# Query and key projections of the first attention: padded stacks replaced by head rows spread through DRAM, with a new order of steps and of filler matmuls

## The reference, cut to what matters

```python
x = x + _L0_xattn_ref(_layernorm(x), ctx_512, ...)   # 16 heads of 8: causal self attention plus attention to the context, then @ Wp
x = x + _L0_ffn_ref(_layernorm(x), ...)              # 8 experts of 512 hidden units, top 2 by a router
x = x + _L1_xattn_ref(_layernorm(x), ctx_512, ctx_512, ...)  # one head of 128, to the context
x = x + _L1_ffn_ref(_layernorm(x), ...)              # 16 heads of 64, values and outputs mixed by top-2 gates over 8 experts
# in _L0_xattn_ref
q = _heads(x @ Wq + bq); k = _heads(x @ Wk + bk)                # self
qc = _heads(x @ Wcq + bcq); kc = _heads(cross_input @ Wck + bck)  # context
```

## Time and profile before

| | us |
|---|---|
| median of 3 runs (lowest, highest) | 1233.53 (1227.9, 1242.0) |
| the profiled execution, its own time | 1238.11 |
| its span | 1236.4 |
| TensorE busy in the span | 1127.7 (91%) |
| DVE, ACT, GpSimd busy | 698.5, 489.9, 84.1 |
| mean granted TensorE clock, as a share of full | 0.939 |

### The profile page before, as it was taken

One profiled execution on the slowest core, in us unless ns is written; L12 is line 12 of the kernel. 1 busy time (PEld: TensorE's weight loads), 2 busy tenths in 40 slices (PEclk: granted clock), 3 DMA queues, 4 the chain that ended last, 5 costly groups with the idle time before them and its releaser, 6 DMA issues.

```text
span 1236.4 us, 22167 instructions
## 1 busy us (share of the span) xinstructions
PE 1127.7 (91%) x8916; PEld 853.0 (69%) x8916; DVE 698.5 (56%) x1867; ACT 489.9 (40%) x1022; POOL 84.1 (7%) x246
## 2 busy tenths in 40 slices
PE   6989979899999999999989999999999999988786
PEld 4547745788569775887578856986578766875475
DVE  5513574856666566746585666747585657424400
ACT  4243406353544525452635344462536163422120
POOL 0020002000100001000200010000100010000000
PEclk9999968999999989999999988999999998998866
DMA  8000001041301421052103230052105210233322
GB/s 227 1 1 5 2 0 37 6 81 41 75 6 27 77 56 42 11 76 70 41 6 72 41 84 6 14 82 65 37 15 77 69 39 1 56 57 82 62 41 56
DMA packets 198037, 56.90 MB, mean 46 GB/s; under 512 B 173569, under 2 KB 193839, under 8 KB 197935
## 3 DMA queue, kind: packets, MB, share of 16 engines
q1 hardware_dynamic: 195630, 51.20, 21.4%
q10 hardware_dynamic: 2304, 4.29, 1.1%
HBM read 31.36 MB, written 24.12 MB: 45 GB/s over the span
## 4 chain that ended last, share of the span: by engine, by line
PE 72%; DVE 11%; ACT 7%; DMA 4%; SPq 3%; issue 3%; ACTq 0%; DVEq 0%
PE bank L985 11%; PE bank L830 9%; PE bank L794 9%; PE bank L900 5%; PE bank L574 5%; PE bank L941 4%; PE bank L720 3%; PE bank L735 3%; PE bank L968 2%; PE bank L645 2%; DMA at<-at_d 2%; PE bank L681 2%; DVE negmax L1322 2%; ACT pa L1079 2%; ACT hi_part L1065 2%
## 5 line engine op out<-in xcount | busy, mean ns | idle before, releaser
L1322 DVE TENSOR_REDUCE negmax<-bank 128x2 f32<-128x512 f32 (+1 forms) x224 | 138.9, 682 | 55.0 <-PE bank L681 35.6
L1079 ACT ACTIVATE pa<-bank 128x512 f32<-128x512 f32 x224 | 123.4, 596 | 109.2 <-PE bank L735 75.9
L1096 ACT ACTIVATE pa<-bank,b_c 128x256 f32<-128x256 f32 x256 | 106.9, 470 | 108.9 <-PE bank L794 106.7
L985 PE MATMUL bank<-vb,pb 128*128 128x65 f32 x1024 | 131.9, 292 | 3.2 <-issue 2.0
L985 PEld LDWEIGHTS bank<-vb,pb 128*128 128x128 f32 x1024 | 128.0, 207 | 9.3 <-ACT pb L1158 3.5
L794 PE MATMUL bank<-xnT_a,w 128*128 128x256 f32 x512 | 124.0, 385 | 1.7 <-ACT pa L1096 1.3
L830 PE MATMUL bank<-w,pa 128*128 128x128 f32 x1024 | 124.2, 276 | 0.0
L830 PEld LDWEIGHTS bank<-w,pa 128*128 128x128 f32 x1024 | 121.9, 192 | 3.2
L574 PE MATMUL bank<-ident 128*128 128x512 bf16 x417 | 117.8, 411 | 0.0
L1158 ACT ACTIVATE pb<-bank 128x512 f32<-128x512 f32 x128 | 69.7, 599 | 111.8 <-PE bank L945 110.8
L794 PEld LDWEIGHTS bank<-xnT_a,w 128*128 128x128 f32 x512 | 92.1, 190 | 17.3 <-ACT pa L1096 4.9
(11 more groups left out here) (241 smaller groups left out, 1715.9 us busy)
## 6 DMA issues: line engine op xcount, KB each, us to landing
v_d<-at SPq DMA_DIRECT2D x32, 256.0 KB, 3.3
vb<-v_d SPq DMA_DIRECT2D x32, 256.0 KB, 5.6
at_d<-at SPq DMA_DIRECT2D x32, 256.0 KB, 2.1
at<-at_d SPq DMA_DIRECT2D x32, 256.0 KB, 4.5
pv_d<-pvs SPq DMA_DIRECT2D x8, 512.0 KB, 2.8
pvs<-pv_d SPq DMA_DIRECT2D x16, 256.0 KB, 4.3
w<-in_L_ffn_W_dram ACTq DMA_DIRECT2D x1, 2048.0 KB, 9.5
bd<-mix_d SPq DMA_DIRECT2D x128, 8.0 KB
```

Source lines behind the costliest of these rows:

```text
L985: mm = pe.matmul(BB[2 + qt][:, i * (DH + 1):(i + 1) * (DH + 1)], pb[:, h % NPB, kt * T + qt * P:kt * T + (qt + 1) * P], vb[:, kt, h, :], s ...
L1079: nc.scalar.activation(pa[:, e % NPA, :], BA[e % 2][:, :], ACT.Exp, scale=SC0).then_inc(S["a_ex"], 1)
L1096: ins = nc.scalar.activation(hT[:, u % 4, c, :], BA[u % 2][:, c * T:(c + 1) * T], ACT.Relu, bias=b1_c[:, k:k + 1])
L1322: nc.vector.tensor_reduce(negmax[:, i:i + ng], BA[j][:, :].rearrange("p (g k) -> p g k", g=ng), AX, ALU.max, negate=True).then_inc(S["a_mx ...
```

## The change

Its parts, as the code has them:

- `w_stack` becomes `w_heads`: weights with columns ordered by channel then head, no repeats. `f_heads` (0: context query and key, 1: self) replaces `f_stack`: 4 matmuls, 4 ACT and 4 DVE instructions for a sequence. SP writes the high parts twice and the low parts once to `q_d` and `k_d` in DRAM (8 DMAs), and `f_spread` reads them back into the strips of `qs` and `ks` (16 DMAs of 25 or 24 rows times 4 heads times 1 KB).
- `f_load`, `f_norm`, `f_norm_apply` move forward (into the scores, before and after the heads); `f_heads` stands before `a_router`; `f_spread` after `a_expert` 4. They have an `xn_f` of their own and two buffers for the context. `x_a` takes the bias early, so `x_f` is free after `a_values`.
- Stream B and its last instance have new orders and places. In `LAST_B`, `b_sel` stands behind both `b_mix`.
- Fillers: the program has 628 instead of 417; in a sequence of the middle `w_norm` 13, `w_third` 7, `w_gather` 23, `w_gates` 6.
- Start: DVE fills `qs` and `ks` once (zeros and the ones row); `last_loads` are issued behind the first `f_spread`; `s_turn` 0 stands behind `a_max` 3.

```diff
-        w_stack = sb("w_stack", [P, 4, G, P])
+        w_heads = sb("w_heads", [P, 4, P])
...
-        qs = sb("qs", [P, 2, G, T], F32R)
-        ks = sb("ks", [P, 2, G, T], F32R)
+        lo_part = sb("lo_part", [P, 4, T], F32R)
+        qs_all = sb("qs", [P, G, 2, T], F32R)
+        ks_all = sb("ks", [P, G, 2, T], F32R)
+        qs, ks = [s[:, :, :, :].rearrange("p g s n -> p s g n") for s in (qs_all, ks_all)]
...
+        ROWS = 3 * D + 1
+        q_d = dram("q_d", [ROWS, H, 2, T])
+        k_d = dram("k_d", [ROWS, H, 2, T])
...
-        KINDS = (Q0, K0, QC, KC)
+        KINDS = (QC, KC, Q0, K0)
...
-        STEPS_A = [("a_values", 0), *run("a_max", 0, 7), ("a_shift", 0), *run("a_score", 0, 14), ("a_lastpv", 0),
-                   ("a_heads", 0), ("a_project", 0), ("a_norm2", 0), ("c_kv", 0), ("a_norm2_apply", 0),
-                   ("a_router", 0), ("a_expert", 0), ("a_expert", 1), ("f_load", 0), *run("a_expert", 2, 6),
-                   ("f_norm", 0), ("a_expert", 6), ("a_expert", 7), ("f_norm_apply", 0), ("a_last", 0),
-                   ("c_norm", 0), ("f_stack", 0), ("c_norm_apply", 0), ("f_stack", 1), ("c_q", 0), ("f_stack", 2),
-                   ("c_max", 0), ("f_stack", 3), ("f_stack", 4), ("c_turn", 0), ("f_stack", 5), ("c_out", 0),
-                   ("f_stack", 6), ("f_stack", 7)]
-        STEPS_B = [("b_norm", 0), ("b_norm_apply", 0), ("b_gates", 0), ("b_top2", 0), *run("b_split", 0, 8),
-                   *run("b_max", 0, 4), ("b_top2", 1), *run("b_max", 4, 8), ("b_top2", 2), ("b_shift", 0),
-                   ("b_fill", 0), ("b_mix", 0), ("b_score", 0), ("b_mix", 1), ("b_score", 1), ("b_sel", 0),
-                   ("b_score", 2), ("b_score", 3), ("b_attend", 0), ("b_score", 4), ("b_score", 5),
-                   ("b_attend", 1), ("b_score", 6), ("b_score", 7), ("b_attend", 2), ("b_attend", 3),
-                   ("b_weigh", 0), ("b_gather", 0), ("b_gather", 1), ("b_out", 0)]
-        AFTER_A = (67, 67, 68, 68, 70, 71, 74, 75, 76, 77, 78, 78, 79, 80, 84, 84, 85, 88, 88, 89, 89, 90, 93, 95,
-                   96, 99, 99, 100, 105, 107, 110, 111, 111, 112, 113, 114, 114, 115, 116, 116, 119, 119, 120)
+        STEPS_A = [("a_values", 0), *run("a_max", 0, 7), ("a_shift", 0), *run("a_score", 0, 8), ("f_load", 0),
+                   *run("a_score", 8, 14), ("f_norm", 0), ("a_lastpv", 0), ("a_heads", 0), ("a_project", 0),
+                   ("f_norm_apply", 0), ("a_norm2", 0), ("c_kv", 0), ("a_norm2_apply", 0),
+                   ("f_heads", 0), ("f_heads", 1), ("a_router", 0), *run("a_expert", 0, 5),
+                   ("f_spread", 0), ("f_spread", 1), *run("a_expert", 5, 8), ("a_last", 0), ("c_norm", 0),
+                   ("c_norm_apply", 0), ("c_q", 0), ("c_max", 0), ("c_turn", 0), ("c_out", 0)]
+        STEPS_B = [("b_norm", 0), ("b_norm_apply", 0), ("b_gates", 0), ("b_split", 0), ("b_top2", 0),
+                   *run("b_split", 1, 8), *run("b_max", 0, 3), ("b_top2", 1), ("b_max", 3), ("b_top2", 2),
+                   *run("b_max", 4, 7), ("b_fill", 0), ("b_max", 7), ("b_shift", 0), ("b_mix", 0), ("b_mix", 1),
+                   ("b_score", 0), ("b_score", 1), ("b_sel", 0), ("b_score", 2), ("b_score", 3), ("b_attend", 0),
+                   ("b_score", 4), ("b_score", 5), ("b_attend", 1), ("b_score", 6), ("b_score", 7),
+                   ("b_attend", 2), ("b_attend", 3), ("b_gather", 0), ("b_weigh", 0), ("b_gather", 1),
+                   ("b_out", 0)]
+        AFTER_A = (60, 63, 64, 66, 66, 67, 71, 72, 73, 76, 76, 78, 83, 86, 86, 87, 88, 90, 90, 90, 91, 91, 91, 94,
+                   95, 96, 96, 101, 102, 102, 103, 103, 103, 104, 105, 106, 106, 107, 108, 111, 112, 112, 113)
...
+        LAST_B = [("b_norm", 0), ("b_norm_apply", 0), ("b_gates", 0), ("b_top2", 0), ("b_split", 0), ("b_top2", 1),
+                   ("b_split", 1), ("b_top2", 2), *run("b_split", 2, 6), ("b_fill", 0),
+                   ("b_split", 6), ("b_split", 7), *run("b_max", 0, 4), ("b_mix", 0), ("b_mix", 1), ("b_sel", 0),
+                   *run("b_max", 4, 8), ("b_shift", 0), *run("b_score", 0, 4), ("b_attend", 0),
+                   ("b_score", 4), ("b_score", 5), ("b_attend", 1), ("b_score", 6), ("b_score", 7),
+                   ("b_attend", 2), ("b_attend", 3), ("b_weigh", 0), ("b_gather", 0), ("b_gather", 1),
+                   ("b_out", 0)]
...
-        WARM_SETUP = 1
-        WARM_FIRST = [10, 4, 4, 14, 11, 7, 4, 9, 5, 6, 0, 13, 6, 3, 4, 3, 2, 2, 13, 0, 7, 0, 1, 6, 0, 3, 4, 5, 0, 0, 0, 0, 2, 1,
-                      3, 0, 1, 0, 0, 0, 2, 1, 2, 9, 11, 15, 4, 11, 0, 16, 14, 3, 6, 2, 10, 7]
-        WARM_LAST = [13, 7, 3, 3, 0, 0, 0, 5, 3, 2, 0, 0, 5, 1, 7, 3, 1, 2, 7, 2, 0, 4, 3, 0, 0, 0, 3, 4, 3, 1, 1, 1, 1, 0, 1,
-                      0, 0, 0, 0, 0, 0, 1, 1]
+        WARM_SETUP = 0
+        WARM_FIRST = [15, 16, 11, 4, 14, 7, 3, 5, 7, 4, 2, 5, 2, 5, 0, 2, 5, 13, 2, 0, 4, 6, 5, 1, 12, 8, 3, 4, 9, 1, 1, 1, 0,
+                      2, 0, 2, 0, 0, 0, 0, 3, 1, 0, 0, 0, 2, 1, 5, 0, 0, 7, 2]
+        WARM_LAST = [9, 0, 0, 3, 0, 4, 2, 6, 0, 4, 2, 3, 0, 0, 0, 3, 3, 1, 2, 6, 5, 0, 2, 2, 5, 7, 3, 0, 2, 5, 3, 0, 0, 0, 0, 0,
+                      0, 0, 0, 3, 5, 0, 0]
         assert len(WARM_FIRST) == len(STEPS_A) and len(WARM_LAST) == len(LAST_B)
...
-        KEPT = dict(w_norm={("c_kv", 0): 5, ("a_router", 0): 5},
-                    w_third={},
-                    w_gather={("a_max", 6): 5, ("b_norm", 0): 1},
-                    w_gates={("a_score", 1): 1, ("a_score", 2): 4, ("b_norm_apply", 0): 1, ("a_score", 3): 1})
+        KEPT = dict(w_norm={("f_norm_apply", 0): 4, ("a_norm2_apply", 0): 1, ("c_kv", 0): 2, ("a_norm2", 0): 6},
+                    w_third={("b_mix", 1): 1, ("c_norm", 0): 4, ("c_q", 0): 2},
+                    w_gather={("b_gather", 0): 7, ("b_norm", 0): 15, ("b_weigh", 0): 15, ("a_max", 5): 9, ("a_max", 6): 7},
+                    w_gates={("b_norm_apply", 0): 3, ("a_score", 2): 1, ("a_score", 3): 2})
...
+            turns = {("a_max", 3): (0,), ("a_max", 4): (1, 2), ("a_max", 5): (3, 4), ("a_max", 6): (5, 6), ("a_shift", 0): (7,)}
             order = [("f_load", 0, 0), ("s_first", 0, 0)] + [("w_first", 0, 0)] * WARM_SETUP
             order += [("f_norm", 0, 0), ("f_norm_apply", 0, 0), ("s_cols", 0, 0)]
-            order += [("f_stack", u, 0) for u in range(4)] + [("s_rows", 0, 0)]
-            order += [("f_stack", u, 0) for u in range(4, 8)] + [("s_bias", 0, 0)]
+            order += [("f_heads", 0, 0), ("f_heads", 1, 0), ("f_spread", 0, 0), ("f_spread", 1, 0),
+                      ("s_last", 0, 0), ("s_rows", 0, 0), ("s_bias", 0, 0)]
...
+                            sp.wait_ge(S["a_xb"], upto("a_xb", 0))
...
+
+                    def s_last(_):
                         for dst, src in last_loads:
                             sp.dma_start(dst, src).then_inc(s_w_last, 16)
+
+                    def s_cols(_):
+                        sp.wait_ge(s_blank, 2)
+                        for sc in range(2):
+                            sp.dma_start(q_d[3 * D, :, sc], qs[0:H, 0, 0, :].bitcast(F32)).then_inc(s_zero_row, 16)
+
+                    def f_heads(half):
+                        for u in (2 * half, 2 * half + 1):
+                            rows_d, kind = (k_d if u % 2 else q_d)[:, :, SELF if half else CROSS], KINDS[u]
+                            first = 0 if u % 2 else D
+                            sp.wait_ge(S["a_mh"], upto("a_mh", u + 1))
+                            sp.dma_start(rows_d[first:first + 2 * D].rearrange("(r d) h n -> (d h) r n", d=D),
+                                         hi_part[:, kind, :].unsqueeze(1).broadcast_to([P, 2, T])).then_inc(S[f"f_hw{half}"], 16)
+                            rest = 2 * D - 2 * first
+                            sp.wait_ge(S["a_split"], upto("a_split", u + 1))
+                            sp.dma_start(rows_d[rest:rest + D].rearrange("d h n -> (d h) n"), lo_part[:, kind, :].bitcast(F32))\
+                                .then_inc(S[f"f_lw{half}"], 16)
+
+                    def f_spread(half):
+                        sc = SELF if half else CROSS
+                        sp.wait_ge(S[f"f_hw{half}"], upto("f_hw0", 32))
+                        sp.wait_ge(S[f"f_lw{half}"], upto("f_lw0", 32))
+                        if now[0] == 0:
+                            sp.wait_ge(s_zero_row, 32)
+                        else:
+                            sp.wait_ge(S["a_st"], upto("a_st", 0))
+                        for j in range(4):
+                            for stack, rows_d, n in ((qs_all, q_d, ROWS), (ks_all, k_d, ROWS - 1)):
+                                sp.dma_start(stack[32 * j:32 * j + n, :, sc, :].bitcast(F32),
+                                             rows_d[0:n].rearrange("r (g j) s n -> j s r g n", j=4)[j, sc])\
+                                    .then_inc(S[f"f_st{half}"], 16)
...
-                    def f_stack(u):
-                        kind = KINDS[u // 2]
-                        if u == 0:
```

(44 more changed lines are left out.)

163 lines of the change are left out of this document (50 added, 113 removed).

## The result

The changed kernel takes 1270.6 us (median of 4; 1266.3 to 1280.2), the kernel before on the same chip 1236.9. The ratio is 1.029, interval 1.024 to 1.035: slower by 3%. The forecast was 1188 with a range up to 1224, so it was wrong; one rival, "SP falls behind", gave 1268.

What follows compares the result with a forecast made beforehand. It took packed TensorE work as the bound, then DVE's queue, half-clock windows and the last B's uncovered waits; -17 - 3 - 7 - 2 - 2 - 5 - 14 = -50 took 1238.1 to 1188 us, range 1160 to 1224.

Steps and rivals of the forecast that it cites:

- SP falls behind: Rival: `f_spread` reads at 1.0 us an issue delay `v_d`; attend 0 waits 11 us in seven sequences; 1268 us, chance 0.06.
- The stage of layer 3: Six middle sequences: removing the stacks gains 7.7 - 1.5 - 1.6 = 4.6 us a sequence, bounds 0 to 6.2.
- near 14: Sign to look for: the stage from the last L830 group to attend 0 takes near 14 us instead of 20.5.
- `f_heads`: Before the experts: its matmuls and ACT and DVE pairs cost +2.4 us a sequence; context and token transposes leaving the experts' stage, -0.6.
- I take these as equal: Around the heads: `f_norm` moved before `a_lastpv` costs what `b_max` 0 and 1 leaving the same stretch save.
- The unread products: Middle sequences: 49 fillers instead of 21, taken as hidden in waits; dips get rarer, -3 us in all (0 to -7).
- SP's queue: Middle sequences: 16 `f_spread` reads at 0.36 us take 5.8 us, hidden before `v_d`; a wait of 0 to 2 us may appear.
- The later landing: At `vb`: by ring order the reads' backlog would delay its landing, losing some 1 to 2 us a sequence.
- First sequence: Layer 3 without stacks -6.5 us, `f_heads` +2.4, fewer fillers between the scores -3.3; together -7.
- The start: `s_turn` 0 moves behind `a_max` 3, but first rows go through DRAM and 26 DMAs precede large loads: -2 us (-6 to +6).
- The last B: `b_sel` behind `v_d` -2 us, gathers at full clock -5 in both, last attends at full clock -14.

Runs made afterwards that it cites:

- held run: The kernel with early reads plus eight more unread products in the waits of the layer 3 stage of the first seven sequences: 1214.9 us.
- early reads: The changed kernel with the 16 `f_spread` reads moved on SP's queue from behind `a_expert` 4 to behind `a_expert` 0: 1218.9 us, 0.989 of before.
- late reads: The changed kernel with both `f_spread` of the middle sequences moved behind `b_sel` of stream B on SP's queue: 1322.7 us, ratio 1.076.

## Why the prediction was wrong

By its own steps:

1. **The stage of layer 3: right, once the wait for `vb` is taken off.** Forecast 4.6 us a sequence; 6.2 less 1.9 for `b_mix` 0 is 4.3 in the held run. In the changed kernel itself the stage less its wait is 13.6 us in every sequence (18.45 less 4.84, for one), where "near 14" was forecast.
2. **`f_heads`: right in its term, incomplete as a sum.** Forecast 2.4 less 0.6. The stretch that I had priced, from the end of `a_lastpv` to the third pair of hidden products, grew from 14.5 us (undisturbed) to 17.0. The reading under it was partly wrong: I took five unread products to go from this stretch, and 13 stand there in place of 10; and the upper bound is 4.0 and not 4.2 (1.9 + 1.14 + 0.96). Not in the sum: 1.1 in the experts where -0.6 was forecast, and 1.3 in gather and scores. "I take these as equal" was written without a row. These 3.0 us cancel the forecast gain of 2.8 a sequence, so the middle without the read problem is that of before (133.7 against 133.5 at an even clock). The experts' 1.1 are the records of `b_max`; DVE's share in the heads is shown; the 1.3 stay open.
3. **The unread products: hidden, as forecast.** 0.4 us a sequence. The dips got rarer, but not in the changed kernel: in six middle periods the windows show 48 us at 1.2 GHz before, 88 after, 17 with early reads, 10 in the held run. At the price of before (2.6 us for each of the three sequences with two dips) that is up to 8 us, where 3 (0 to 7) was forecast. What made them rarer isn't shown: with 18 fewer unread products it is still only 14 us.
4. **SP's queue: the step that failed.** I priced a read of 1 KB pieces at 0.36 us by the issues of `bd`, and it took 0.77. With 0.36 the block would have been 5.8 us; it was 12.9. The bounds were at hand: the earlier trace rows show 0.36 and 1.0, and the rival with 1.0 us put the turning point at 0.8. I chose the lower end because the piece count was like that of `bd`, but `bd`'s rows move 8 KB a DMA and these 100, over 25 partitions. Two more things were missed. The rival counted 11 us of wait and none of clock; it was 4.2 of wait and 3.9 of clock, 53 us in all in place of its 80, and 25 us were lost elsewhere: its 1268 was luck. And the earlier trace rows, which I had read as a matter of the start, was a second part of the mechanism: reads in flight lengthen the issues behind them. `v_d`'s four issues take 4.08 us, and 1.85 with early reads. Of the 4.3 us by which `vb` is later behind `b_mix` 1 (6.0 against 1.7), these are 2.2, and the block of reads is the rest. The 0.77 itself is no backlog: the first read takes 0.81 us and the last 0.78. The later landing by "1 to 2 us" was too little: at 4 KB, where SP had time, the backlog alone left waits of 2.6 to 4.7 us in four sequences. There `vb` is issued 2.7 us later than with early reads, and 2.0 of them are the two issues of `v_d` behind `b_mix` 1 (1.92 and 0.91 in place of 0.36 and 0.50). The Trainium skill, DMA: Bandwidth & Descriptors, "Queues, rings and completion order", has the ring order that I had weighed; the run with 4 KB pieces and 25 rows agrees, but shows the delay at the issue too, where I had excluded it.
5. **First sequence: right.** From the first score to the first token product of the next sequence it takes 86.8 us, 96.7 before: -9.8 where -7 was forecast.
6. **The start: wrong in size.** The first score comes at 65.0 in place of 56.4, so +8.6 where -2 (-6 to +6) was forecast. Of these, 4.9 stand ahead of `a_max` 0, which waits 4.85 us for `ks`, the stack that now goes through DRAM, with the clock low behind it; that wait was in no term of the sum. The loads of layer 4 are issued at 36.4, behind the first 16 reads, and `s_turn` 0 waits 1.49 us for them. The run with the turns moved got 3.2 us back.

```profile
33.25 0.80 PE L711 MATMUL bank<-ks,qs 32*128 32x256 f32 x8 [4.85 <-DMA ks<-k_d]
36.41 0.52 SPq L476 DMA_DIRECT2D pb<-in_L_ffn_Wq_dram  x1
```

7. **The last B: right.** -21 forecast, -23.4 measured, and the full clock in the attends is as drawn. The run with only `b_sel` moved gives most of it: the order on SP counts more than the products between the scores. The Trainium skill, TensorE: Matmul & The Clock Gate, "HAM oscillation — how this bites in real kernels", says that a stream whose bursts stand between waits for DMA falls to half clock again and again; the windows behind the waits for `vb` and `ks` agree (0.50).

Against the sum of -50: up to the first attend 0 the forecast was -9 and +2.9 came, 4.2 of it the first wait for `vb`; the last B -21 and -23.4; the six middle sequences -20 and +48.7, of which 8.1 x 6 = 48.6 is step 4. The miss is 78 us on the span (+28.2 for -50): 53 are step 4 (the six periods and the first wait for `vb`), 20 the middle, where the forecast gain did not come, 10.6 the start, less 2.8 in the first sequence and 2.4 in the last B.

## What to carry to other kernels

A DMA issue must be priced by a row with its own shape (partitions, piece size, bytes), and where the rows span a factor of three, the dear end belongs in the forecast, not in a rival. New issues go into a stretch where the queue waits anyway: against the early place, the same 16 reads cost 0, 8 or 17 us a sequence by where they stood. Stages are to be compared between sequences whose granted clock is even, since dips on one side hide or feign a gain. And each wait of TensorE is to be priced twice, once as itself and once as the half clock behind it, which was about as large as the wait or, with late reads, several times that.

## What the runs showed of the hardware

An issue on SP of a read from DRAM took 0.73 to 0.81 us for 25 or 24 partitions with four pieces of 1 KB each, 0.60 for 32 partitions of the same, 0.30 for 25 or 24 pieces of 4 KB and 0.42 for 32 of them. Reads of 4 KB pieces over 25 and 24 partitions in flight made the next issues two to five times as long (1.92 and 0.91 us for 0.36 and 0.50), with the 16 DMA engines busy for 0.52 of the time at 141 GB/s; reads of 4 KB pieces over 32 partitions with a third more bytes did not (0.36 and 0.61 us), at 1.03 and 226 GB/s. With 1 KB pieces over 32 partitions the issues behind were still as long as 1.30 us. Waits as short as 0.56, 0.70 and 0.66 us within 10 us were followed by the clock at 1.2 GHz in two of six sequences, and in no sequence of the seven runs that have eight unread products in them.
